# Attention's second half: exponentials and value copies ahead of operations that wait for loads, scans later, next queries' load ahead of the wait for sends

## What is computed

```python
def reference(x, fside, cond, ...):
    r = bi_wkv(x, fside, fside, w, u, cond)       # first gate: two scans over the rows, forward and back
    q, k, v = r @ Wq + bq, r @ Wk + bk, r @ Wv + bv     # q is reshaped to (b, h, t, dh) without a transpose
    logits = einsum('bhtd,bhds->bhts', q, k) / sqrt(128)
    weights = softmax(logits + causal_mask)
    x = x + einsum('bhts,bhsd->bhtd', weights, v) @ Wo + bo
    g = bi_wkv(x, fside, fside, w, u2, cond)      # second gate = sigmoid(x) * f2(fside): rows x2
    scores = sigmoid(g @ gate_w)                  # then: top 2 of 4 groups, top 6 of the experts left
    return x + experts(g) + shared(g)
```

## Time and profile before

| | us |
|---|---|
| median of 3 runs | 2274.76 |
| lowest and highest of them | 2269.83, 2284.47 |
| the profiled execution, whole | 2294.18 |
| its span | 2292.5 |
| PE busy in the span | 2138.1 (93%) |
| DVE, ACT, POOL busy | 1354.1 (59%), 1159.8 (51%), 1439.5 (63%) |
| turns 8 to 15 of the attention, from the first matmul of turn 8's scores | 656.2 to about 1204 |

### The profile page before, as it was taken

How to read it: one execution, slowest core, us unless ns; L and a number is a source line. 1 busy time by engine, 2 the same in 40 slices (tenths; PEclk the granted TensorE clock), 3 DMA queues, 4 the chain that set the end, 5 groups by cost and what they waited for, 6 DMA issues and landing times. The chain is left out here.

```text
span 2292.5 us, 39958 instructions
## 1 busy us (share of the span) xinstructions
PE 2138.1 (93%) x11247; PEld 1855.4 (81%) x11247; DVE 1354.1 (59%) x2499; ACT 1159.8 (51%) x2491; POOL 1439.5 (63%) x961
## 2 busy tenths in 40 slices
PE   2899999999999999989889889999999999999996
PEld 1678888888878878777777679988999999998975
DVE  8868888888756676766765443333333333333386
ACT  4477777777767777767653123333333333333310
POOL 7887787787755656666672212466677777753365
PEclk9989999999999999999998899999999999999998
DMA  5444444533365546665435534556667676664566
GB/s 129 140 121 127 135 134 164 161 105 121 115 221 170 170 131 195 216 207 167 132 126 208 202 117 128 159 166 189 186 191 210 188 208 186 197 196 133 172 200 208
DMA packets 367657, 380.29 MB, mean 166 GB/s; under 512 B 51556, under 2 KB 283560, under 8 KB 362728
## 3 DMA queue, kind: packets, MB, share of 16 engines
q1 hardware_dynamic: 255608, 252.20, 35.7%
q10 hardware_dynamic: 96496, 75.28, 10.6%
q0 software_dynamic: 15360, 50.34, 6.7%
HBM read 264.21 MB, written 120.59 MB: 168 GB/s over the span
## 5 line engine op out<-in xcount | busy, mean ns | idle before, releaser
L2089 POOL TENSOR_SCALAR we_high<-we_raw 128x1408 fp32r<-128x1408 f32 (+1 forms) x94 | 132.3, 1407 | 317.9 <-PE up_e L684 230.3
L2091 POOL TENSOR_TENSOR we_low<-we_raw,we_high 128x1408 fp32r<-128x1408 f32 (+1 forms) x94 | 312.3, 3322 | 7.8
L2304 DVE TENSOR_TENSOR hidden_e<-silu_e,up_e 128x352 f32<-128x352 f32 x127 | 66.2, 522 | 248.8 <-ACT silu_e L2243 248.8
L2287 DVE TENSOR_TENSOR hT_low<-hT_ps,hT_high 128x256 fp32r<-128x256 f32 x127 | 53.9, 425 | 253.0 <-ACT hT_high L2229 246.6
L2243 ACT ACTIVATE silu_e<-gate_e 128x352 f32<-128x352 f32 x127 | 59.1, 465 | 282.4 <-PE up_e L684 271.1
L684 PE MATMUL gate_e<-we_high,xT_high 128*128 x508 | 176.1, 347 | 11.5 <-DVE xT_low L2294 6.4
L2248 ACT ACTIVATE rows_out<-down_e 128x512 f32<-128x512 f32 x127 | 76.1, 599 | 198.8 <-PE down_e L684 196.1
L684 PE MATMUL gate_e<-we_high,xT_low 128*128 x508 | 164.3, 323 | 0.0
L684 PE MATMUL up_e<-we_high,xT_high 128*128 x508 | 163.9, 323 | 0.0
L684 PE MATMUL gate_e<-we_low,xT_high 128*128 x508 | 163.9, 323 | 0.0
L684 PE MATMUL up_e<-we_high,xT_low 128*128 x508 | 163.6, 322 | 0.0
(11 more groups left out here) (402 smaller groups left out, 7191.2 us busy)
## 6 DMA issues: line engine op xcount, KB each, us to landing
slots_out<-rows_out ACTq DMA_DIRECT2D x127, 256.0 KB
rows_early<-slots_in ACTq DMA_DIRECT2D x500, 64.0 KB
we_raw<-L_ffn_w_gate SPq DMA_DIRECT2D x32, 704.0 KB, 4.8
we_raw<-L_ffn_w_up SPq DMA_DIRECT2D x32, 704.0 KB, 5.0
w_ring<-L_attn_Wq SPq DMA_DIRECT2D x64, 256.0 KB
q_T<-q_out SPq DMA_DIRECT2D x64, 256.0 KB, 2.4
w_ring<-L_attn_Wk SPq DMA_DIRECT2D x64, 256.0 KB
w_ring<-L_attn_Wv SPq DMA_DIRECT2D x64, 256.0 KB
```

What stands on the lines that cost most here:

```text
L2089: nc.gpsimd.tensor_scalar(wh[:, p, at:to], raw[:, at:to], 1.0, 1.0, ALU.mult, ALU.mult).then_inc(w_hi, 1)
L2091: nc.gpsimd.tensor_tensor(wl[:, p, at:to], raw[:, at:to], wh[:, p, at:to].bitcast(F32), ALU.subtract).then_inc(w_split, 1)
L2304: nc.vector.tensor_tensor(hb[:], sg[:], psu[:], ALU.mult).then_inc(h_done, 1)
```

## The change

Only the tables of the orders are changed; no instruction of a tile is added or taken away, and no buffer. PE's and POOL's lists stay as they are.

```diff
 ACT_ORDER (phase 1, then phase 2)
-    "u u mG mS0 E0 mH0 u u V0 V1 N0 E1 V2 r2 V3 hk a0 mR0 u r3 Q0 ...
-    "u mG u u E0 V0 r2 N0 V1 u V2 a0 hk u mS0 E1 V3 mH0 b0 r3 K2 u N1 ...
+    "u u mG E0 V0 mS0 V1 N0 mH0 u u E1 V2 r2 V3 hk a0 mR0 u r3 Q0 ...
+    "u mG E0 V0 u u r2 N0 V1 u V2 a0 hk u E1 V3 mS0 b0 r3 mH0 K2 u N1 ...
 DVE_ORDER
-    "M0 mX0 mD0 i0 V0 M1 V1 V2 i1 mW0 V3 ... mP2 mP3 hb mA1 M3 a2 A1 i3 b2 ...
-    "M0 mD0 i0 V0 V1 V2 a0 M1 mD1 mX0 hm V3 b0 mW0 i1 K2 mD2 K3 ...
+    "M0 i0 V0 mX0 mD0 V1 M1 V2 i1 mW0 V3 ... mP2 M3 mP3 mA1 a2 A1 i3 hb b2 ...
+    "M0 i0 V0 mD0 V1 V2 a0 M1 mD1 V3 hm b0 i1 mX0 K2 mW0 mD2 K3 ...
 SP_ORDER (phase 2)
-    "Ny o f u x0 W u u u y0 w0 x1 v0 u u v1 u lq y1 U u U U U U w1".split(),
+    "Ny o f u x0 W u u u y0 w0 x1 v0 u u u lq u v1 y1 U U U U w1".split(),
```

More of the change, by code:

```diff
@@ L408 @@
     "u E0 u V0 u u N0 V1 u V2 a0 gx E1 V3 b0 r2 N1 Q0 u K2 u hk r3 a1 he A0 b1 u Q1 E2 K3 gc N2 u A1 u Q2 u a2 u E3 b2 k0 N3 Q3 a3 A2 gk u k1 b3 u u A3 u ge h0 h1".split(),
-    "u u mG mS0 E0 mH0 u u V0 V1 N0 E1 V2 r2 V3 hk a0 mR0 u r3 Q0 u u he N1 b0 K2 mS1 a1 u Q1 u A0 mH1 K3 E2 u b1 Q2 u N2 mR1 A1 a2 E3 b2 N3 Q3 u u a3 A2 b3 u k0 k1 u A3 h0 u h1".split(),
-    "u mG u u E0 V0 r2 N0 V1 u V2 a0 hk u mS0 E1 V3 mH0 b0 r3 K2 u N1 K3 mR0 u he A0 u a1 E2 b1 mS1 k0 N2 E3 a2 A1 b2 N3 u mH1 a3 A2 mR1 b3 k1 u A3 h0 u h1 u".split(),
+    "u u mG E0 V0 mS0 V1 N0 mH0 u u E1 V2 r2 V3 hk a0 mR0 u r3 Q0 u u he N1 b0 K2 mS1 a1 u Q1 u A0 mH1 K3 E2 u b1 Q2 u N2 mR1 A1 a2 E3 b2 N3 Q3 u u a3 A2 b3 u k0 k1 u A3 h0 u h1".split(),
+    "u mG E0 V0 u u r2 N0 V1 u V2 a0 hk u E1 V3 mS0 b0 r3 mH0 K2 u N1 K3 mR0 u he A0 u a1 E2 b1 mS1 k0 N2 E3 a2 A1 b2 N3 u mH1 a3 A2 mR1 b3 k1 u A3 h0 u h1 u".split(),
 )
@@ L413 @@
     "M0 ga i0 V0 gb V1 V2 M1 a0 i1 V3 gd gr b0 gR K2 hm a1 M2 gf A0 b1 i2 K3 ha A1 M3 a2 hb i3 b2 k0 a3 A2 hd b3 k1 gm A3 O0 O1 hr hR hf O2 O3".split(),
-    "M0 mX0 mD0 i0 V0 M1 V1 V2 i1 mW0 V3 hm a0 mD1 mA0 mD2 b0 K2 ha mX1 a1 M2 K3 mW1 A0 mP0 i2 mP1 b1 mP2 mP3 hb mA1 M3 a2 A1 i3 b2 hd a3 A2 b3 k0 k1 A3 hr O0 hR O1 hf O2 O3".split(),
-    "M0 mD0 i0 V0 V1 V2 a0 M1 mD1 mX0 hm V3 b0 mW0 i1 K2 mD2 K3 M2 a1 mA0 A0 mP0 i2 mP1 b1 mP2 mP3 M3 mX1 k0 ha i3 a2 A1 b2 hb mW1 a3 A2 b3 k1 A3 mA1 hd O0 hr O1 hR O2 hf O3".split(),
+    "M0 i0 V0 mX0 mD0 V1 M1 V2 i1 mW0 V3 hm a0 mD1 mA0 mD2 b0 K2 ha mX1 a1 M2 K3 mW1 A0 mP0 i2 mP1 b1 mP2 M3 mP3 mA1 a2 A1 i3 hb b2 hd a3 A2 b3 k0 k1 A3 hr O0 hR O1 hf O2 O3".split(),
+    "M0 i0 V0 mD0 V1 V2 a0 M1 mD1 V3 hm b0 i1 mX0 K2 mW0 mD2 K3 M2 a1 mA0 A0 mP0 i2 mP1 b1 mP2 mP3 M3 mX1 k0 ha i3 a2 A1 b2 hb mW1 a3 A2 b3 k1 A3 mA1 hd O0 hr O1 hR O2 hf O3".split(),
 )
@@ L424 @@
     "x0 u Ny u o u u f w0 y0 v0 s0 u x1 W s1 u u u w1 y1 s2 u s3 u u lq u U v1 U U U".split(),
-    "Ny o f u x0 W u u u y0 w0 x1 v0 u u v1 u lq y1 U u U U U w1".split(),
+    "Ny o f u x0 W u u u y0 w0 x1 v0 u u u lq u v1 y1 U U U U w1".split(),
 )
```

## The result

The changed kernel takes 2292.52 us (median of 4 runs, 2290.79 to 2298.5), the kernel before 2275.55 (median of 4): ratio 1.0074, 95% interval 1.0049 to 1.0098. It is 17 us slower, where 12 us faster was forecast, and outside the range of 2247 to 2277. Its profiled execution took 2298.5 us.

What follows compares the result with a forecast made beforehand. PE, busy 93% of the span, was taken as the bound. Turns 8 to 14 summed as 3.2 - 1.2 + .3 - 1.8 + 2 + 5.5 + 4 = 12.0 us, from 2274.76 to 2263; range 2247 to 2277.

Steps and rivals of the forecast that it cites:

- `s2` on POOL waits up to 5 us longer for `hb` ... and I take 0: Turns 8 to 11: POOL's sums wait for late scans; hidden by some 3 us of slack, otherwise up to .5 each turn.
- Turn 9: The clean case: E1's uncovered table load makes Xy wait 1.4, .2 of it there anyhow; -1.2 us.
- Turn 12, "+2": K3's 3.02 wait, its clock and others go, 4.6 for PE, but DVE's list at b1 leaves a gain of +2 us.
- free edit: `mX0`, `mD0` behind V0 on DVE: M1 comes later by nothing, because S1 isn't done; no cost counted.
- `Xy`'s wait: Turns 8 to 11: new PE idle time behind ACT's later E1; 2.0, 1.4, 1.6 in turns 8 to 10, 4 in 11.
- turn 10, "+.3": New Xy wait -1.6, against 1.9 of b2's 2.78 won by moving the scans; sum +.3 us.
- S1 of turns 8 and 11: PE's waits of 2.96 and 2.14 for E0 go, with the lower clock behind them: 5.2 and 4.3 us gained.
- b2 of turn 10: PE's 2.78 wait for DVE, whose scans stand ahead of M3: 1.9 of it goes.
- V2 of turns 13 and 14: PE's waits of 3.54 and 3.11, behind two `u` waiting for K3's weights, go: +5.5 and +4 us.
- the prediction's last sentence: Forecast most easily wrong by turns 8 to 11, nearly cancelling, and DVE's order in turns 12 to 14, not priced row by row.
- Rival 4: A table switch between E0 and E1 costs 1.28 more, 10 us together in four turns: 2273; chance .05.
- Rival 3: Slower: Xy's wait reaches some 3 us in turns 8 to 11, dropping PE's clock each time: 2277 or 2283; chance .06.

Runs made afterwards that it cites:

- hb_only: The kernel before with only DVE's late scans in turns 8 to 11 (M3 ahead of mP3, hb behind i3): 2301.87 where before takes 2288.34, 1.0067.
- p1_only: The kernel before with only the ACT and DVE lists of turns 8 to 11 changed: 2286.46, ratio 1.0029.
- act1_only: The kernel before, turns 8 to 11 only: ACT's E0 and V0 ahead of mS0, DVE's mX0 and mD0 behind V0, M1 behind V1; scans unmoved: 2297.46, 1.0032.
- p2_only: The kernel before with only the ACT, DVE and SP lists of turns 12 to 15 changed: 2288.12, ratio 1.0046.
- sp_only: The kernel before with only SP's list of turns 12 to 15 changed (next queries and last units ahead of v1): ratio .9987.
- md0_only: The kernel before with one item moved, mD0 behind i0 and V0 on DVE in turns 12 to 15: 2294.98 where before takes 2288.34, 1.0034.
- p2_keep: The kernel before with SP's new list and, on ACT in turns 12 to 15, E0 and V0 ahead of the two u: ratio .9989.
- best1: The kernel before with SP's new list, E0 and V0 ahead of two u (turns 12-15), M3 and a2 ahead of mP3 and hb (turns 8-11): .9988.
- p1_ms0_late: The kernel before, turns 8 to 11: the chunk's sigmoid behind E1 and V2 on ACT, mX0 behind V2 on DVE; scans as before: ratio .9993.

## Why the prediction was wrong, step by step

- **"`s2` on POOL waits up to 5 us longer for `hb` ... and I take 0"** is the first step that failed. I looked for who waits for POOL's weights behind `s2` and found slack, and not for who waits for `s2` itself: `hd` on DVE, .55 behind it in turn 9 already. The delay was 7 us, DVE stood 4.94, PE lost 1.49 and .86. Turns 8 to 11 average 296.2 in five profiles with all of phase 1 changed and 288.8 in three with the scans back or unmoved: 7.4 us. Turn 9 shows this best: -1.2 was forecast, -1.4 is what it loses with the scans back, and the late scans take 2.0 more. In the whole time the scans' part is shown only alone (hb_only, .67%, turn 12's hold included); p1_only, which is act1_only with the late scans added, is at .29% against .32%, since turns 12 and 14 of its profile are 4.5 and 3.4 shorter.
- **Turn 12, "+2"**, came out as -10.6 against the one profile before. K3's 3.02 went as reckoned (PE made up 4.9 on before at that point, 4.6 forecast). What I had not priced is `mD0`'s new place: I counted it as a free edit with `mX0`, since M1 wasn't due. V1, V2 and `Xy` were what stood behind it. Its instructions are short, but their time depends on POOL's. The two experiments on this item put it at 7.9 (taken back) and 5 to 10.5 us (alone, by which profile it is compared with) in turn 12, part of it PE's lower clock: behind `Xy`'s 4.25 the matmuls of 128x512 start .43 apart (969 to 970), and .87 is the turn's mean clock. L0's 2.42 behind `k_low`, which stands behind the later `mW0` and `mD2`, is a further miss, still there when `mD0` is back (3.11).
- **`Xy`'s wait** was sized well: 1.4, 2.0 and 1.6 forecast for turns 9, 8 and 10; 1.47, 1.46 and 2.42 measured. In turn 11 I took the cautious end, 4; it is 1.47, near the 1.1 of the end that I had not chosen. What was mis-sized is turn 10, "+.3": ACT's order alone made it 5.2 longer (act1_only), 3.1 of that slower matmuls, which the term left out.
- **S1 of turns 8 and 11**: gone, with 5.1 and 4.3 made up at V2, as forecast. Turn 8's is there in every profile with the same lists (72.4 to 75.3 us). Turn 11's is a property of that one execution: with the same lists it took 68.6 to 71.4 us in p2_only, sp_only, md0_only and p2_keep, against the 72.9 of the earlier trace rows. So is turn 13's wait at V2, as shown above. The two were 4.3 and 5.5 us of the forecast's gains. A stall at a late load, read from a single profile, is not the mean.
- **b2 of turn 10**: 2.15 won, 1.9 forecast. **V2 of turns 13 and 14**: 6.1 and 3.5 won there, 5.5 and 4 forecast; then given back within the turn. In turn 13, b1 waits 1.95 and the matmuls behind it ran at half clock; in turn 14 three instructions of `mD0` are held for 1.59, 1.15 and 1.19 and `Xy` waits 2.05. The loads came as reckoned: `q_high` waits for `q_raw` in none of turns 12 to 14. So the sum of turns 12 to 14 was wrong by what comes next in line, as the prediction's last sentence feared.
- **The rivals.** Rival 4 is out: no gap at a switch. Rival 3 had the sign and nearly a cause (`Xy` in the lower clock), but its place was ACT and turns 8 to 11; ACT's part is 2 us of the turns there, and of its mechanism only turn 10 shows something. Its premise, that a wait of 2.78 to 3 drops the clock, was misread: the earlier trace rows stand behind the 2.96; behind the 2.78 of turn 10 and the 3.11 of turn 14 in the same profile the matmuls start .23 apart. In act1_only eight matmuls behind the 2.77 at the same place are .43 apart.
- **Measured against one profile.** Before's profiled execution was .85% above the median. Its 12 extra us lie behind the attention: from the next stage's first matmul to the span's end it takes 1084.1 us, the changed kernel's 1072.1. The difference of the attentions, 16.6, is near that of the medians, 17.0, but this is in part luck, since before's turns were long too: turns 8 to 14 take 491.2 in it, and 483.1 to 488.4 in the four runs whose time is that of before or slightly less (sp_only, p2_keep, best1, p1_ms0_late). They take 507.3 in the changed kernel.

On the hold, the Trainium skill, "SBUF — State Buffer", section "Who interferes with whom", says that VectorE and GpSimd share a pair of SBUF ports, which one of them holds exclusively; that casts and tensor_scalar in a two-port mode, and instructions with two inputs in SBUF while GpSimd reads SBUF, can contend for it; that tensor_reduce on this chip never does; and that an instruction with at most one SBUF input does not outside the two-port modes. The kinds agree with these traces: CAST, TENSOR_SCALAR and TENSOR_TENSOR were held, TENSOR_REDUCE took .16 in the midst of a run. The length doesn't follow from that page: it speaks of a hold for one instruction, and here it lasted through four or five of POOL's. That the ports are the reason is taken from the page; the runs show only the kinds and the times.

## What to carry to other kernels

Before an item is moved, follow its result to the next engine and on to whoever waits there, and ask of every item that now stands behind it, however short its own instructions are; the two edits counted as free here were some three quarters of the loss. Here short VectorE instructions on SBUF operands were only short while GpSimd had no run of ready work, so keep such instructions off the path, or leave a gap in GpSimd's run. Look in the profile for an instruction that takes .17 in one place and 2 in another, even where it costs nothing yet. And a stall at a load in one profiled execution should be discounted: compare several executions of the same lists before it enters a sum.

## What the runs showed of the hardware

An instruction of 8 or 16 columns on DVE took up to 7.11 us (.17 where it wasn't held), and ended .03 or .04 us behind POOL's run in all six cases of the table. It was held also where it began up to .7 us ahead of the run, while POOL was still in its last send (hb_only, md0_only). Elsewhere DVE was let in after each single operation of POOL (changed kernel, turn 14: 1.59, 1.15, 1.19), or after one operation of a longer run (`hd` at 785.15, 1.48 us). What decides between one and five isn't settled. PE's idle times of 1.47 at `Xy` in turns 9 and 11 left it at a granted clock of 1.00 over the turn; those of 4.25 and 5.73 brought half clock behind them. Between them the length of the idle time doesn't decide: behind the same 2.77 or 2.78 at b2 of turn 10 the matmuls of 128x512 start .23 apart in the kernel before and .43 apart in act1_only.
